# Convolution block, image loop: the output stores moved from SyncE's queue to ScalarE's

## Chip, cores, metric

One Trainium2 chip, one of its cores. The metric is the device time of one execution in microseconds (us); the median of three runs is quoted. All other times are from one profiled execution, counted from the start of its span.

## What is computed

The input `x` has 8 images of 64 channels of 224 x 224 float32. Cut to what matters:

```python
x = x + conv_block(group_norm(x, 32 groups))
# inside conv_block:
res = conv3x3(x, W_id, b_id)                      # all 8 images
# image 0 alone: wavelet split, two attentions, conv3x3 over 256 channels
out = leaky_relu(conv3x3(dmt, W_enc, b_enc), 0.01)   # one map, shape (1, 64, 224, 224)
return out + res                                  # the map is added to every image
```

## The kernel before, in words

The program has three stages, one after another on every engine: `before_maps` (statistics of image 0, weights, row filter), `encoder` (the one map of image 0, kept in SBUF as `e_map`, and the statistics of the other images) and `main` (the image loop, lines 1425 to 1694). The change touches `main` alone. It runs from about 795 us to the end.

**Tiling of `main`.** An image is cut into `NB` = 14 bands. A band has 8 rows of the upper and 8 rows of the lower half of the image: channels of the upper half lie on partitions 0 to 63, those of the lower half on 64 to 127. With the halo a band is 10 rows of 224 elements per partition. The 8 images make 112 bands, numbered n = 14 i + b. Band n goes through these steps:

- `load` (L1488, DMAs at L1499): two DMAs of 64 x 2240 float32 (560 KB) bring the band to `xs[slot]`. There are six slots: bands 1 to 12 share four of them in turn, band 0 has one and band 13 has one of its own.
- `high` and `full` on ScalarE (L1511, L1518): the float16 high part of the normalized band, and the whole of it in float32. `high` of band n waits until the convolution of band n - 2 is through (`tiles`). `split` on VectorE (L1522) makes the float16 low part.
- `conv` on TensorE (L1587): 216 matmuls of 64 x 64 by 448 columns. TensorE's program is written out for all 112 bands; those of SyncE, ScalarE, VectorE and GpSimd are a hardware loop over the images.
- `read_out` on VectorE (L1654): eight instructions scale the PSUM tiles and add `x` from `xs`; each counts `evac` up by one. They write `stage[b % 2]`, and wait first until the store of band n - 2 has landed (`stored`).
- GpSimd (L1681) adds `e_map` in four instructions per band; each counts `added` up by one.
- `store` (L1616): when all four additions are done, four DMAs of 224 KB write the band out.

**SyncE's order.** SyncE issues all transfers of the loop in the written order store(b), load(b + 4). ScalarE issues none. Here `AHEAD` is 4:

```python
for b in range(NB):
    store(i, b)
    load(sp, i, b + AHEAD) if b + AHEAD < NB else load(sp, i + 1, b + AHEAD - NB)
```

**What a load waits for.** Besides its place in the queue, a load waits for the read-out of the band that was last in its slot (`last_band`, L1482):

```python
if b in (TOP, BOTTOM):
    return NB * i + b - NB
return NB * i + b - 4 if b > 4 else NB * i + b - 6
```

So bands 5 to 12 wait for the read-out of bands 1 to 8 of the same image; bands 13 and 0 wait for that of their namesake one image before; bands 1, 2, 3 and 4 wait for that of bands 9, 10, 11 and 12 of the image before. The first loads (bands 0 to 3 of image 0) are issued at the end of the encoder's part of SyncE, and the first two bands are also prepared there.

Of the kernel before, what the change touches and what calls it, by code (L numbers as in the profile page):

```python
# [15 lines left out]
B, C, H, W = 8, 64, 224, 224  # L16
# [10 lines left out]
NB = HALF // R  # L27
# [131 lines left out]
def conv_preact(nc, t, out):  # L159
# [4 lines left out]
    with ExitStack() as top:  # L164
# [29 lines left out]

        with ExitStack() as mid:
            images, ahead = main(nc, x, out, psum, sb, sem, top, pool_of, early, e_map, partner, mv_all, norm_all, w_hi, w_lo, w_max)
            shared = [sb(mid, f"shared{k}", [P, NI * 3 * C]) for k in range(2)]
            weff = [m[:, :].bitcast(F16).rearrange("p (s i y e) -> p s i y e", s=2, i=NI, y=3) for m in shared]
# [1226 lines left out]
def main(nc, x, out, psum, sb, sem, top, pool_of, early, e_map, partner, mv_all, norm_all, w_hi, w_lo, w_max):  # L1425

    with ExitStack() as s5:
# [17 lines left out]
        stage = [sb(s5, f"stage{i}", [P, 2, 2, NT]) for i in range(2)]  # L1445
# [19 lines left out]
        added = sem(top, "added")  # L1465
        stored = [sem(top, f"stored{i}") for i in range(2)]
# [8 lines left out]
        def slot_of(b):  # L1475
            return {TOP: 4, BOTTOM: 5}.get(b, (b - 1) % 4)
# [5 lines left out]
        def last_band(i, b):  # L1482
# [5 lines that stand above are left out]
        def load(sp, i, b):  # L1488
            slot = slot_of(b)
            sp.wait_ge(evac, 8 * (NB + last_band(i, b) + 1))  # L1490
            for s in (1, 0):
                lo_row, hi_row = 0, RH
                if b == TOP and s == 0:
                    lo_row = 1
                if b == BOTTOM and s == 1:
                    hi_row = RH - 1
                row0 = HALF * s + R * b - 1
                src = x[bass.ds(i, 1), :, row0 + lo_row:row0 + hi_row, :]
                sp.dma_start(xs[slot][C * s:C * s + C, lo_row * W:hi_row * W],  # L1499
                             src.rearrange("a c h w -> (a c) (h w)")).then_inc(x_in[slot], 16)  # L1500

        def take_norm(act, i):
            act.wait_ge(xn_ready, NB * i + 1)
            act.copy(norm_now, norm_all[:, bass.ds(i, 1), :].rearrange("p a b -> p (a b)")).then_inc(norm_taken, 1)
            act.wait_ge(norm_taken, i + 1)
# [5 lines left out]
        def high(act, i, b):  # L1511
            n, p, slot = NB * i + b, b % 2, slot_of(b)
            act.wait_ge(x_in[slot], 32 * uses(i, b) + 32)
            act.wait_ge(tiles, 2 * n + 2)
            act.activation(x_hi[p][:, :, 1:1 + W], xs[slot].rearrange("p (r w) -> p r w", w=W), ACT.Identity,  # L1515
                           scale=norm_now[:, 0:1], bias=norm_now[:, 1:2]).then_inc(hi_ready, 1)

        def full(act, i, b):  # L1518
            act.wait_ge(lo_ready, NB * i + b + 1)
            act.activation(xn, xs[slot_of(b)], ACT.Identity, scale=norm_now[:, 0:1], bias=norm_now[:, 1:2]).then_inc(xn_ready, 1)  # L1520
# [92 lines left out]
            pool.tensor_tensor(root, gvar, half7, ALU.pow).then_inc(root_ready, 1)  # L1613

        def sync(sp):
            def store(i, b):  # L1616
                p = b % 2
                sp.wait_ge(added, 4 * (NB * i + b) + 4)
                for s in range(2):
                    for k in range(2):  # L1620
                        row0 = HALF * s + R * b + 4 * k
                        dst = out[bass.ds(i, 1), :, row0:row0 + 4, :]
                        sp.dma_start(dst.rearrange("a c h w -> (a c) (h w)"), stage[p][C * k:C * k + C, s, :, :].rearrange("c g n -> c (g n)"))\
                          .then_inc(stored[p], 16)

            AHEAD = 4
            with sp.Fori(0, B - 1) as i:
                for b in range(NB):
                    store(i, b)
                    load(sp, i, b + AHEAD) if b + AHEAD < NB else load(sp, i + 1, b + AHEAD - NB)  # L1630
            for b in range(NB):
                store(B - 1, b)
                if b + AHEAD < NB:
                    load(sp, B - 1, b + AHEAD)
            for p in range(2):
                sp.wait_ge(stored[p], 64 * (B * NB // 2 + 1))

        def scalar(act):
            def prep(i, b):
                high(act, i, b)  # L1640
                full(act, i, b)

            act.wait_ge(normed, 1)
            with act.Fori(0, B - 1) as i:
                for b in range(2, NB):
                    prep(i, b)
                take_norm(act, i + 1)
                for b in range(2):
                    prep(i + 1, b)
            for b in range(2, NB):  # L1650
                prep(B - 1, b)

        def vector(dve):
            def read_out(i, b):  # L1654
                n, p, slot = NB * i + b, b % 2, slot_of(b)

                dve.wait_ge(stored[p], 64 * (n // 2 if isinstance(n, int) else 7 * i + b // 2) + 64)
                for g in range(2):
                    dve.wait_ge(tiles, 2 * n + g + 5)
                    for r in range(2):  # L1660
                        for k in range(2):
                            o, lanes = slice(C * k, C * k + C), slice(C * r, C * r + C)
                            c = (1 + 4 * k + 2 * g) * W
                            dve.scalar_tensor_tensor(stage[p][o, r, g, :], psum[4 * p + 2 * g + r][o, 0:NT], w_max[lanes, 0:1],  # L1664
                                                     xs[slot][lanes, c:c + NT], ALU.mult, ALU.add).then_inc(evac, 1)

            with dve.Fori(0, B - 1) as i:
                for b in range(NB):
                    read_out(i, b)
                    split(dve, i, b + 2) if b + 2 < NB else split(dve, i + 1, b + 2 - NB)  # L1670
            for b in range(NB):
                read_out(B - 1, b)
                if b + 2 < NB:
                    split(dve, B - 1, b + 2)
# [6 lines left out]
        def gpsimd(pool):  # L1681
            with pool.Fori(0, B) as i:
                for b in range(NB):
                    n, p = NB * i + b, b % 2
                    for g in range(2):
# [6 lines left out]
        ahead = Ahead(load=lambda sp, b: load(sp, 0, b), dummies=dummies, pads=pads, norms=norms, norm_first=first_norm,  # L1692
                      high=high, full=full, split=split, edges=edges, root=root_of, partners=partners, conv=conv)
        return Programs(sync, tensor, scalar, vector, gpsimd), ahead


# [40 lines left out]
```

## Time and profile before

| what | value |
|---|---|
| median of three runs | 1970.77 us (1967.54 to 1971.35) |
| the profiled execution: its time | 1965.66 us |
| its span | 1963.7 us |
| busy TensorE (PE) | 1934.4 us, 99% |
| busy VectorE (DVE) | 1464.4 us, 75% |
| busy ScalarE (ACT) | 1008.3 us, 51% |
| busy GpSimd (POOL) | 1032.8 us, 53% |
| data DMA queue (q1) | 387.10 MB, 77.2% of 16 engines |
| instruction DMAs (q8) | 278 packets, 4.55 MB |

How to read it: PE is TensorE's matmuls and PEld its weight loads, which overlap them; SPq is SyncE's queue of DMA issues. An idle time is put down to what ended it; "issue" means that nothing the profile knows of did. PEclk is the share of full clock that TensorE was granted. q1 holds the data that SyncE's DMAs move, q8 the packets that bring instructions to the engines.

### The profile page before, as it was taken

Reading aid. Unit: us, or ns where it says so; the run is one execution under the profiler, and the core shown is the slowest. Engines: PE = TensorE matmul, PEld = TensorE weight load, DVE = VectorE, ACT = ScalarE, POOL = GpSimd, SP = SyncE. Lnnn points to the kernel's source line nnn. Section 1 sums busy time; section 2 is a strip of 40 time slices with the busy share of each in tenths; the row PEclk is TensorE's granted clock in tenths of the full one; section 3 lists DMA queues with packets and bytes.
Section 4 is the critical chain, followed back from the end, with each engine's and each line's share of the span. In section 5 each row is a group of like instructions: output and inputs, shape, how many; then the busy total and the mean of one; then the engine's idle time right before and its main releaser. Section 6 shows DMA issues by size and latency. Waiting matters only on the chain.

```text
span 1963.7 us, 79515 instructions
## 1 busy us (share of the span) xinstructions
PE 1934.4 (99%) x35530; PEld 1609.5 (82%) x35530; DVE 1464.4 (75%) x2253; ACT 1008.3 (51%) x1067; POOL 1032.8 (53%) x775
## 2 busy tenths in 40 slices
PE   8999999999999999999999999999999999999998
PEld 7987999999999999668897888767877778766664
DVE  5665578778878876577777777777777777777776
ACT  4555666666666676634444344434444444444432
POOL 0005878887888885444444444444444444444444
PEclk9999999999999999999999999999999999999999
DMA  8883598888888884588888877887887878877774
GB/s 172 238 289 98 166 276 214 218 214 216 209 219 215 209 215 104 134 202 205 198 205 208 199 204 197 207 200 194 201 210 198 200 202 206 204 201 199 206 207 124
DMA packets 132647, 391.92 MB, mean 200 GB/s; under 512 B 49676, under 2 KB 50448, under 8 KB 118128
## 3 DMA queue, kind: packets, MB, share of 16 engines
q1 hardware_dynamic: 132336, 387.10, 77.2%
q8 instruction: 278, 4.55, 1.0%
q14 instruction: 33, 0.27, 0.1%
HBM read 258.56 MB, written 128.45 MB: 197 GB/s over the span
## 4 chain that ended last, share of the span: by engine, by line
PE 36%; issue 33%; POOL 26%; ACT 1%; DVE 1%; DMA 1%; POOLq 1%; SPq 0%; DVEq 0%; ACTq 0%
POOL stage L1689 26%; PE ps L1097 13%; PE ps L1063 7%; PE ps L621 5%; PE ps L1067 5%; PE ps L1066 3%; PE ps L623 3%; POOLq L1687 1%; DMA big<-in_x 1%; DVE pool_of L1284 0%; DVE pool_of L1272 0%; DMA pool_of<-in_x 0%; POOL pool_of L1358 0%; POOL pool_of L315 0%; POOL pool_of L306 0%
## 5 line engine op out<-in xcount | busy, mean ns | idle before, releaser
L1689 POOL TENSOR_TENSOR stage<-stage,big 128x448 f32<-128x448 f32 x448 | 511.5, 1142 | 642.7 <-DVE stage L1664 639.9
L1601 PE MATMUL ps<-pool_of,w_hi 64*64 64x448 f16 x12096 | 645.9, 350 | 3.7 <-issue 3.3
L1601 PEld LDWEIGHTS ps<-pool_of,w_hi 64*64 64x64 f16 x12096 | 450.4, 107 | 147.3 <-issue 8.7
L1601 PE MATMUL ps<-pool_of,w_lo 64*64 64x448 f16 x8064 | 452.4, 350 | 2.2 <-issue 2.2
L1601 PEld LDWEIGHTS ps<-pool_of,w_lo 64*64 64x64 f16 x8064 | 304.5, 107 | 98.3 <-issue 4.8
L1664 DVE SCALAR_TENSOR_TENSOR stage<-ps,w_max,pool_of 64x448 f32<-64x448 f32 x448 | 305.9, 683 | 45.7 <-PE ps L1601 33.0
L1284 DVE BATCH_NORM_STATS2 pool_of<-big 128x6 f32<-128x448 f32 x392 | 232.5, 617 | 76.8 <-DMA big<-in_x 76.6
L1515 ACT ACTIVATE pool_of<-pool_of 128x2240 f16<-128x2240 f32 x56 | 126.4, 2258 | 313.9 <-PE ps L1601 313.9
L1664 DVE SCALAR_TENSOR_TENSOR stage<-ps,w_max,xs 64x448 f32<-64x448 f32 x384 | 262.1, 683 | 33.5 <-PE ps L1601 22.1
L1515 ACT ACTIVATE pool_of<-xs,pool_of 128x2240 f16<-128x2240 f32 x48 | 108.4, 2258 | 284.4 <-PE ps L1601 284.4
L1601 PE MATMUL ps<-big,w_hi 64*64 64x448 f16 x4032 | 225.4, 350 | 0.0
L1063 PE MATMUL ps<-pool_of 112*128 112x246 f16 x1344 | 218.8, 271 | 1.0 <-DVE d_odd L1272 0.5
L1067 PE MATMUL ps<-pool_of 112*128 112x168 f16 x1344 | 217.8, 243 | 0.0
L1526 DVE TENSOR_TENSOR big<-pool_of 128x2240 f16<-128x2240 f32 x56 | 139.8, 2496 | 93.4 <-ACT pool_of L1520 93.4
L1526 DVE TENSOR_TENSOR pool_of<-pool_of 128x2240 f16<-128x2240 f32 x56 | 139.7, 2495 | 90.7 <-ACT pool_of L1520 90.7
L1066 PE MATMUL ps<-pool_of 112*128 112x90 f16 x1344 | 201.3, 206 | 0.0
L1601 PEld LDWEIGHTS ps<-big,w_hi 64*64 64x64 f16 x4032 | 153.4, 107 | 46.2
L621 PE MATMUL ps<-fh,pool_of 112*112 112x238 f32 (+1 forms) x512 | 145.6, 366 | 10.8 <-DMA pool_of<-in_x 8.3
L1097 PE MATMUL ps<-pool_of,shared 128*64 128x224 f16 x3024 | 148.4, 259 | 1.2 <-issue 1.2
L1097 PE MATMUL ps<-d_odd,shared 128*64 128x224 f16 x3024 | 148.3, 259 | 0.9 <-issue 0.6
L1097 PEld LDWEIGHTS ps<-pool_of,shared 128*64 128x64 f16 x3024 | 143.7, 110 | 3.0 <-issue 1.4
L1097 PEld LDWEIGHTS ps<-d_odd,shared 128*64 128x64 f16 x3024 | 143.8, 110 | 2.6 <-issue 0.8
(197 smaller groups left out, 2487.4 us busy)
## 6 DMA issues: line engine op xcount, KB each, us to landing
out<-stage SPq DMA_DIRECT2D x448, 224.0 KB, 3.2
big<-in_x SPq DMA_DIRECT2D x392, 224.0 KB, 5.2
pool_of<-in_x SPq DMA_DIRECT2D x104, 560.0 KB, 7.0
xs<-in_x SPq DMA_DIRECT2D x96, 560.0 KB, 7.1
pool_of<-row_filtered SPq DMA_DIRECT2D x110, 224.0 KB, 3.8
pool_of<-in_x SPq DMA_DIRECT2D x32, 392.0 KB, 7.4
row_filtered<-big SPq DMA_DIRECT2D x2, 6272.0 KB, 22.7
row_filtered<-big SPq DMA_DIRECT2D x4, 1568.0 KB, 8.9
```

The source lines that it names most:

```text
L621: pe.matmul(o[:, 0:width], xg[g][:, near, c % CG, :], fh[:, near, first:first + width], start=True, stop=False)
L623: pe.matmul(far_out, xg[g][:, far, c % CG, :], last_rows(fh[:, far, :], first, reach), start=False, stop=True).then_inc(product, 1)
L1063: pe.matmul(tiles(o)[:, :, 15:NTILE], lhs[:, 1, a, :], tiles(v)[:, :, 15:NTILE], start=(k == 0), stop=False)
L1066: pe.matmul(tiles(o)[:, :, 0:15], lhs[:, 0, a, :], tiles(v)[:, :, 0:15], start=False, stop=False)
L1067: mm = pe.matmul(both(o), lhs[:, 0, a, :], both(v), start=False, stop=(k == 2))
L1097: mm = pe.matmul(o[s], weff[a][:, sw, i, ky, :], d[n][:, b, r:r + 4, sw, NTILE * i:NTILE * i + NTILE], start=(k == 0), stop=(k == len(piec ...
L1284: ins = dve.bn_stats(records[:, 2 * (k % CHN) + i, :], sx[k % 4][:, i * NT:i * NT + NT])
L1515: act.activation(x_hi[p][:, :, 1:1 + W], xs[slot].rearrange("p (r w) -> p r w", w=W), ACT.Identity, scale=norm_now[:, 0:1], bias=norm_now[ ...
L1526: ins = dve.tensor_tensor(x_lo[p][:, :, 1:1 + W], xn.rearrange("p (r w) -> p r w", w=W), x_hi[p][:, :, 1:1 + W], ALU.subtract)
L1601: mm = pe.matmul(psum[4 * p + 2 * g + r][C * k:C * k + C, 0:NT], w[lanes, t, :], v[lanes, y:y + 2, kx:kx + W], start=(j == 0), stop=(j == ...
L1664: dve.scalar_tensor_tensor(stage[p][o, r, g, :], psum[4 * p + 2 * g + r][o, 0:NT], w_max[lanes, 0:1], xs[slot][lanes, c:c + NT], ALU.mult, ...
L1689: pool.tensor_tensor(stage[p][:, r, g, :], stage[p][:, r, g, :], e_map[:, e:e + NT], ALU.add)\
```

## The change

ScalarE issues the stores, from its own DMA queue. Those of band b - 2 stand behind `high` and `full` of band b; the last two bands of an image stand behind the preparation of the next image's bands 0 and 1, and those of the last image stand at the end. SyncE's loop holds the loads alone, in the same order as before, and its last waits for `stored`. Buffers, semaphores, DMA shapes and every wait of a load and of a store are unchanged.

```diff
         def sync(sp):
+            AHEAD = 4
+            with sp.Fori(0, B - 1) as i:
+                for b in range(NB):
+                    load(sp, i, b + AHEAD) if b + AHEAD < NB else load(sp, i + 1, b + AHEAD - NB)
+            for b in range(AHEAD, NB):
+                load(sp, B - 1, b)
+            for p in range(2):
+                sp.wait_ge(stored[p], 64 * (B * NB // 2 + 1))
+
+        def scalar(act):
             def store(i, b):
                 p = b % 2
-                sp.wait_ge(added, 4 * (NB * i + b) + 4)
+                act.wait_ge(added, 4 * (NB * i + b) + 4)
...
-                        sp.dma_start(...)
+                        act.dma_start(...)
                           .then_inc(stored[p], 16)
-            AHEAD = 4
-            with sp.Fori(0, B - 1) as i:
-                for b in range(NB):
-                    store(i, b)
-                    load(sp, i, b + AHEAD) if b + AHEAD < NB else load(sp, i + 1, b + AHEAD - NB)
...
             with act.Fori(0, B - 1) as i:
                 for b in range(2, NB):
                     prep(i, b)
+                    store(i, b - 2)
                 take_norm(act, i + 1)
                 for b in range(2):
                     prep(i + 1, b)
+                    store(i, NB - 2 + b)
             for b in range(2, NB):
                 prep(B - 1, b)
+                store(B - 1, b - 2)
+            for b in range(NB - 2, NB):
+                store(B - 1, b)
```

## Rows read from the trace of the kernel before

**Rows 1.** The page's head, and its PE and PEld rows: busy us, instructions

```profile
span 1963.7 us, 79515 instructions
...
PE 1934.4 (99%) x35530; PEld 1609.5 (82%) x35530; DVE 1464.4 (75%) x2253; ACT 1008.3 (51%) x1067; POOL 1032.8 (53%) x775
...
q8 instruction: 278, 4.55, 1.0%
```

**Rows 2.** Waits between 830 and 1964 us: total us, times, longest us

```profile
ACT pool_of L1515 <- PE ps L1601: 636.1, 108, 7.3
...
PE ps L1601 <- issue: 3.5, 7, 1.1
```

**Rows 3.** Timeline of one band: start us, us, engine, line, what

```profile
1200.37 2.26 ACT L1515 ACTIVATE pool_of<-xs,pool_of 128x2240 f16<-128x2240 f32 x1 [5.84 <-PE ps L1601]
1200.38 2.83 DVE L1664 SCALAR_TENSOR_TENSOR stage<-ps,w_max,pool_of 64x448 f32<-64x448 f32 x4 [0.45 <-PE ps L1601]
...
1202.54 2.24 ACT L1520 ACTIVATE pool_of<-xs,pool_of 128x2240 f32<-128x2240 f32 x1
...
1203.28 1.14 POOL L1689 TENSOR_TENSOR stage<-stage,big 128x448 f32<-128x448 f32 x1 [0.29 <-DVE stage L1664]
...
1204.58 2.53 SPq L1623 DMA_DIRECT2D out<-stage  x4
1204.81 2.49 DVE L1526 TENSOR_TENSOR pool_of<-pool_of 128x2240 f16<-128x2240 f32 x1 [1.60 <-ACT pool_of L1520]
...
1207.34 2.83 DVE L1664 SCALAR_TENSOR_TENSOR stage<-ps,w_max,xs 64x448 f32<-64x448 f32 x4
1207.42 1.30 SPq L1499 DMA_DIRECT2D pool_of<-in_x  x2
...
1210.62 2.26 ACT L1515 ACTIVATE pool_of<-big,pool_of 128x2240 f16<-128x2240 f32 x1 [5.84 <-PE ps L1601]
```

**Rows 4.** SyncE's store line: count, ns min/median/max of one

```profile
L1623 SPq DMA_DIRECT2D out<-stage x448: 466/518/1814, 812.8 to 1960.1; - x150
L1623 SPq FUSED_REGOPS  x392: 37/37/48, 812.6 to 1815.6; - x196
L1623 SPq MOVE out<-stage x392: 29/29/38, 812.7 to 1815.7; - x196
```

**Rows 5.** DMA view, 830 to 1964 us: packets, MB, share; issues, us to landing

```profile
q1 hardware_dynamic: 52294, 222.58, 77.9%
q8 instruction: 184, 3.01, 1.2%
...
out<-stage SPq DMA_DIRECT2D x440, 224.0 KB, 3.2
...
xs<-in_x SPq DMA_DIRECT2D x92, 560.0 KB, 7.0
```

**Rows 6.** DMA view, 792.9 to 804.2 us, then 804.2 to 806 us

```profile
q1 hardware_dynamic: 234, 1.76, 71.4%
issues: line engine op xcount, KB each, median us to landing
pool_of<-in_x SPq DMA_DIRECT2D x2, 560.0 KB, 6.3
xs<-in_x SPq DMA_DIRECT2D x2, 560.0 KB, 11.4
...
q8 instruction: 1, 0.02, 4.7%
```

**Rows 7.** Windows after 805.2 us: length, busy us (x count), PEclk, DMA share

```profile
805.20:807.20 2.00, 0.01 (x3) 0.00 (x0) 0.00 (x0) 1.41 (x3) 0.31 (x1) 1.00 0.79 161
807.20:810.70 3.50, 3.50 (x40) 1.87 (x44) 2.08 (x4) 2.17 (x2) 2.62 (x3) 0.51 0.03 10
810.70:820.00 9.30, 9.30 (x204) 5.75 (x199) 5.96 (x7) 2.31 (x3) 3.86 (x4) 1.00 0.61 160
```

**Rows 8.** PE at 1321 us; DMA view, 1309.1 to 1318.4, then 1318.4 to 1320

```profile
1321.31 0.76 PE L1601 MATMUL ps<-pool_of,w_hi 64*64 64x448 f16 x11 [1.09 <-issue]
...
q1 hardware_dynamic: 464, 2.03, 90.0%
...
q8 instruction: 1, 0.02, 5.1%
```

**Rows 9.** Encoder, 448 to 466 us: its window, and its DMA view

```profile
448.00:466.00 18.00, 18.00 (x319) 17.45 (x317) 15.14 (x25) 11.92 (x17) 15.18 (x9) 1.00 0.92 220
...
q8 instruction: 2, 0.03, 0.9%
...
big<-in_x SPq DMA_DIRECT2D x16, 224.0 KB, 5.3
```

More of the change, by code:

```diff
@@ L1622, in store @@
                         dst = out[bass.ds(i, 1), :, row0:row0 + 4, :]
-                        sp.dma_start(dst.rearrange("a c h w -> (a c) (h w)"), stage[p][C * k:C * k + C, s, :, :].rearrange("c g n -> c (g n)"))\
+                        act.dma_start(dst.rearrange("a c h w -> (a c) (h w)"), stage[p][C * k:C * k + C, s, :, :].rearrange("c g n -> c (g n)"))\
                           .then_inc(stored[p], 16)
-            AHEAD = 4
-            with sp.Fori(0, B - 1) as i:
-                for b in range(NB):
-                    store(i, b)
-                    load(sp, i, b + AHEAD) if b + AHEAD < NB else load(sp, i + 1, b + AHEAD - NB)
[L1631 to L1638, printed above, removed]
             def prep(i, b):
```

## Prediction

> **What bounds the kernel now.** I read the page's head first: TensorE is busy for 1934.4 of 1963.7 us [rows 1]. In the waits of the image loop ScalarE stands 636.1 us waiting for TensorE's matmuls, and TensorE itself lacks only 3.5 us in seven gaps, all put down to "issue" [rows 2]. The timeline of one band gives the period and everyone's room: ScalarE's `high` starts at 1200.37 and again at 1210.62, so a band takes 10.25 us, all of it matmuls [rows 3]. In phases after the end of a convolution (1200.37 = 0): the read-out ends at 2.8, ScalarE's preparation at 4.4, GpSimd's last addition at 4.05, the stores are issued from 4.2 to 6.7, VectorE's split runs from 4.4 to 6.9, the loads are issued from 7.05 to 8.35, and the next `high` is due at 10.25 [rows 3]. No engine but TensorE sets the pace, and a gain can come only out of TensorE's gaps.
>
> So I looked at what the gaps are. There are 278 instruction packets of 4.55 MB in all, against 2 x 35530 = 71060 matmuls and weight loads [rows 1]: 256 of them per packet, one packet per 6.2 us of the loop (184 in 1134 us, [rows 5]). The packets are TensorE's code. Around the gap at 1320.22 to 1321.31 no code packet starts for 9.3 us while the data queue is 90% busy; one then starts between 1318.4 and 1320, and TensorE goes on [rows 8]. The longest gap, 1.99 us up to 807.2, has the same form: SyncE issues four loads of 560 KB in that stretch, no code packet starts for 11.3 us, one starts behind 804.2 [rows 6]. The loads issued last land after 11.4 us, against 7.0 in the steady loop [rows 5, 6]. **Code waits behind data, and TensorE then waits for code.** 9.3 us without code cost 1.1 us and 11.3 cost 2.0: some 8.2 to 9.3 us between packets are free, that is 2 to 3 us of delay. After the 2-us gap the granted clock was 0.51 (the 1.2 GHz level) for 3.5 us, in which 40 matmuls were done where 204 x 3.5/9.3 = 77 would have been: 37/21.9 = 1.7 us more [rows 7]. One such event costs 2.0 + 1.7 = 3.7 us.
>
> **The change, part by part.**
>
> *Issuing on ScalarE.* Per band four DMA issues with two register instructions each: 4 x (518 + 37 + 29) ns and gaps, 2.53 us in the row [rows 3, 4]. They begin at about 4.4 and end at 6.9; ScalarE has nothing else until 10.25. With SyncE's worst issue, 1814 ns, in all four it would be 7.3 us and end at 11.7, 1.4 us late. I take 2.5 us, hidden under ScalarE's wait of 5.84 us: zero. The copy of the next image's norms moves behind them by as much: zero. The tail has the same four issues behind the same addition: zero. ScalarE's loop body grows by 14 x 12 = 168 issue and register instructions and 14 waits; a pause at its loop's end has 3.3 us of ScalarE's own room. Zero, once per image.
>
> *The new wait on ScalarE.* `added` of band n - 2 now stands ahead of `high` of band n + 1. It is met at 4.4 at the latest and `high` is due at 10.25. VectorE is the one that waits for ScalarE, TensorE behind it (split ends at 6.9, its matmuls start at 10.25). Zero.
>
> *The stores.* Issued 0.2 us later, now beside the loads. They must have landed when VectorE starts to write the same `stage` buffer two bands on, at 6.97 + 10.25 = 17.2; the last goes out at 6.3 and takes 3.2 [rows 3, 5]: 7.7 us of room. Zero, unless a burst (below) holds them.
>
> *The loads, steady part.* What held them was SyncE's store in front. Now only `evac` does: they go out at about 3.0 instead of 7.05. Two loads (1.15 MB) and four stores (0.92 MB) come within 4.1 us. At 252 GB/s of a busy queue (222.58 MB in 77.9% of 1134 us, [rows 5]) 1.0 MB of it is moved by then, so some 1.1 MB or 4.4 us of data stand ahead of a code packet from phase 4.3 to 7.1 and over 3 us until about 8.5, where today this lasts 1.5 to 2 us behind the loads. Today that costs 3.5 us in the loop [rows 2]; two to three times as long a stretch gives 5 more. Bounds: 0 (nothing stalls more) and, with a 0.5-us stall in 4 of 10 bands, 22. I take 8.
>
> *The loads, bursts.* This is the large term. Today the stores pace the loads, one band each. In the new order load 12 waits for the read-out of band 8, and loads 13 and 0 behind it wait for nothing that is still open. Six DMAs, 3.44 MB or 13.7 us of data, are issued within 4 us, once in each of seven images; then nothing for two bands. Four such DMAs cost 3.7 us [rows 6, 7]. The two more are 4.6 us of data. Lower bound 3.7 (what counts is only what the four showed), upper 3.7 + 4.6 = 8.3; a code packet is due every 6.2 us, so one always falls into it. I take the middle, 6: 7 x 6 = 42 us. The last image has only loads 12 and 13 together: 0 to 3.7, I take 2. At the start load 4 follows the four loads of [rows 6] at once, where it stood behind the first store (812.8, [rows 4]): 0 to 4.6, I take 2.
>
> *The sum:* 42 + 2 + 2 + 8 = **+54 us**. The profiled execution took 1965.66 us, 5.1 below the median of 1970.77, so 2019.7 for its like and **2025** for the median. This case's own range: 7 x 3.7 = 26, and less where a burst misses, from 1990; upper 7 x 8.3 + 3.7 + 4.6 + 22 = 88, 2060.
>
> **The rivals.** 0.2% (4 us) is what a measurement can tell from no change.
>
> *A, code gets through: no slowdown, 1971.* In the encoder 18 us at a DMA share of 0.92 pass with two code packets and not one gap of TensorE [rows 9]; so a full queue alone does not starve it. There the DMAs are of 224 KB, and few are outstanding (they land in 5.3 us). If the wait of a code packet is limited by its turn and not by the data queued, bursts cost nothing beyond today's, and two queues may even give it turns sooner. It decides at 2 to 3 us of delay: below that everything is hidden. Then the time is 1971 less 0 to 4. Against it stands the 11.3 us without code behind four loads [rows 6].
> The Trainium skill (DMA: Bandwidth & Descriptors, Queues, rings and completion order) says that each DMA engine goes round-robin between its queue rows, a packet at a time. By that rule a code packet would wait for one packet of each row, and the change would cost nothing; the trace does not agree, with 11.3 us in which none started. I give A 0.24.
>
> *B, faster.* Loads that start 4 us earlier could end the gaps: at most all 3.5 us of [rows 2] and the 3.7 at the start, 1964. It would need the code to wait less with more data queued. 0.04.
> The Trainium skill (Perfetto Trace Analysis, DMA Optimizations) recommends one issuing engine for inputs and another for outputs where there are loops; here no load is waited for, so the rule has nothing to win but these gaps.
>
> *C, ScalarE becomes the bound.* If an issue takes over (10.25 - 4.4)/4 = 1.46 us on it; at 1.81 each 1.4 us x 111 = 155 us, 2126. The median of 518 ns speaks against it. 0.03.
>
> *D, the stores starve.* Behind a burst of 4.4 MB with the stores (17 us) a store could land up to 21 us after the convolution's end, 4 us past VectorE's need; VectorE has 0.45 + 1.60 idle and 3.3 us ahead of TensorE, so it decides at 5. A little beyond it: 2 us x 7, added to the forecast: 2039. 0.04, inside the range.
>
> **How the numbers follow.** The forecast has 0.65, A 0.24, B 0.04, C 0.03, D 0.04. Faster: B, and the edge of A: 0.05. Same: most of A, 0.22. Slower: 0.73. The range goes down to A, 1969, and up to 2062; it leaves out C, B and the ends of the forecast.
>
> **What would show it.** Right: TensorE's "issue" gaps in the loop rise from 3.5 us to 30 or more, the long ones (over 2 us) once per image beside six loads in a row, each followed by a stretch at half clock, with loads landing after 11 us and more; ScalarE's issues at 0.5 to 0.6 us each and its wait for TensorE still about 3 us. Wrong: bursts are there and code packets start among them; or ScalarE's issues are long; or VectorE waits for DMAs to `out`.

## The result, and the profile after

The changed kernel takes 1994.15 us (1990.8 to 1997.0, 4 runs), the kernel before 1969.15 us with its profiled run counted in. The ratio is 1.0125, 95% interval 1.0106 to 1.0145: **25 us slower**, clear of the 0.2% bound. The forecast was 2025 us, +54. The sign and the mechanism came out; the size was twice too large. Of run 8 below one execution in six took 4110 us, which no trace here explains, and its ratio leaves that one out.

The page of the changed kernel, for [rows 1] and the table of before:

```profile
span 1993.8 us, 79515 instructions
...
PE 1943.5 (97%) x35530; PEld 1549.1 (78%) x35530; DVE 1465.9 (74%) x2253; ACT 1008.0 (51%) x1067; POOL 1039.5 (52%) x775
...
q1 hardware_dynamic: 96496, 284.31, 56.5%
q10 hardware_dynamic: 35840, 102.79, 15.5%
q8 instruction: 278, 4.55, 1.0%
```

The stores are now q10, ScalarE's queue. The bytes and the 278 code packets are the same. The profiled execution took 1995.58 us, 29.9 more than that of before. TensorE's busy time is 9.1 us longer for the same 35530 matmuls, and its idle time is 21 us longer.

The waits of the changed kernel in the image loop, 830 to 1994 us (as in [rows 2]: total us, times, longest us):

```profile
POOL stage L1691 <- DVE stage L1666: 652.1, 440, 8.8
ACT pool_of L1515 <- PE ps L1601: 629.1, 106, 10.5
...
PEld ps L1601 <- issue: 37.5, 36, 3.2
PE ps L1601 <- issue: 22.7, 23, 2.8
ACT pool_of L1504 <- issue: 20.9, 7, 3.5
DVE stage L1666 <- DMA out<-stage: 20.7, 7, 4.5
ACT pool_of L1515 <- POOL stage L1691: 13.9, 2, 7.1
```

TensorE's gaps have gone from 3.5 to 22.7 us, all "issue" as before. Its weight loads tell more, since a recorded matmul is 350 ns long and covers part of a gap: theirs went from 9.4 to 37.5, by 28.1, which is nearly all of the 29.9 us between the two profiled executions. (The PEld row of before, over the image loop:)

```profile
PEld ps L1601 <- issue: 9.4, 16, 1.5
```

Two waits are new: VectorE for stores, once per image, and ScalarE's `high` for the additions, twice. The row of L1504 is no wait: the profile doesn't count DMA issues as busy, and ScalarE issues the four stores right in front of the copy of the norms. It is so in all seven images; in image 0:

```profile
935.76 3.18 ACTq L1633 DMA_DIRECT2D out<-stage  x4
...
939.16 0.19 ACT L1504 COPY pool_of<-norm_all 128x2 f32 x1 [3.20 <-issue]
```

The timeline of the changed kernel in the burst of image 0 (columns as in [rows 3]):

```profile
898.54 1.74 SPq L1499 DMA_DIRECT2D xs<-in_x  x2
899.75 2.77 ACTq L1633 DMA_DIRECT2D out<-stage  x4
...
900.54 1.47 SPq L1499 DMA_DIRECT2D big<-in_x  x2
902.32 19.04 SPq L1499 DMA_DIRECT2D pool_of<-in_x  x6
...
910.70 2.85 PE L1601 MATMUL ps<-pool_of,w_hi 64*64 64x448 f16 x55 [0.66 <-issue]
...
914.39 5.68 DVE L1666 SCALAR_TENSOR_TENSOR stage<-ps,w_max,pool_of 64x448 f32<-64x448 f32 x8 [1.67 <-DMA out<-stage]
...
917.01 2.26 ACT L1515 ACTIVATE pool_of<-xs,pool_of 128x2240 f16<-128x2240 f32 x1 [6.82 <-POOL stage L1691]
...
919.76 3.21 PE L1601 MATMUL ps<-pool_of,w_hi 64*64 64x448 f16 x36 [2.79 <-issue]
```

Loads of three bands go out one after another from 898.5 us. TensorE stops twice within 12 us, for 0.66 and 2.79 us. The DMA view of the changed kernel, 898.8 to 907.9 us, and 908 to 916.9 us below it, has no q8 row in either stretch:

```profile
q1 hardware_dynamic: 235, 1.69, 64.2%
q10 hardware_dynamic: 213, 0.65, 25.5%
...
q1 hardware_dynamic: 277, 1.94, 84.4%
q10 hardware_dynamic: 123, 0.34, 16.5%
```

So code packets start at about 907.9 and 917.0, and TensorE goes on 2.8 us behind each. The bursts do in kind what was forecast. Within 28 us of the first load of a burst lie 16.9 of the 22.7 us of the matmuls' gaps and 24.2 of the 37.5 us of the weight loads'. What the bursts did to the landing times shows in the same kernel over the loop:

```profile
out<-stage ACTq DMA_DIRECT2D x441, 224.0 KB, 6.6
...
xs<-in_x SPq DMA_DIRECT2D x92, 560.0 KB, 6.5
...
big<-in_x SPq DMA_DIRECT2D x8, 504.0 KB, 9.6
pool_of<-in_x SPq DMA_DIRECT2D x7, 504.0 KB, 15.2
```

The last row is band 0 of the next image, the third of a burst. Stores land after 6.6 us in place of 3.2 [rows 5]. It is the loads beside them and not the other queue: in run 1, where the loads wait for the stores' issue, they land after 3.1 us from ScalarE's queue too.

### The profile page after: what moved, and what is told of

Same layout as the page of the kernel before. It is cut to its first block, busy times and chain, and to the rows that moved or that the text cites. A ratio compares the mean times of both kernels' runs of the same rounds, so it can differ in the third digit from the quotient of the medians.

```text
span 1993.8 us, 79515 instructions
## 1 busy us (share of the span) xinstructions
PE 1943.5 (97%) x35530; PEld 1549.1 (78%) x35530; DVE 1465.9 (74%) x2253; ACT 1008.0 (51%) x1067; POOL 1039.5 (52%) x775
## 4 chain that ended last, share of the span: by engine, by line
PE 37%; issue 33%; POOL 26%; ACT 1%; POOLq 1%; DVE 0%; DMA 0%; SPq 0%; DVEq 0%; ACTq 0%
POOL stage L1691 26%; PE ps L1097 14%; PE ps L1063 7%; PE ps L621 5%; PE ps L1067 5%; PE ps L1066 3%; PE ps L623 3%; POOLq L1689 1%; DMA pool_of<-in_x 0%; POOL pool_of L315 0%; POOL pool_of L306 0%; PE ps L587 0%; POOL pool_of L1358 0%; ACT pool_of L1151 0%; PE ps L513 0%
## 5 line engine op out<-in xcount | busy, mean ns | idle before, releaser
L1691 POOL TENSOR_TENSOR stage<-stage,big 128x448 f32<-128x448 f32 x448 | 518.2, 1157 | 662.3 <-DVE stage L1666 659.6
L1601 PE MATMUL ps<-pool_of,w_hi 64*64 64x448 f16 x12096 | 647.0, 351 | 15.2 <-issue 15.1
L1601 PEld LDWEIGHTS ps<-pool_of,w_hi 64*64 64x64 f16 x12096 | 416.2, 107 | 194.3 <-issue 22.2
L1601 PEld LDWEIGHTS ps<-pool_of,w_lo 64*64 64x64 f16 x8064 | 282.9, 107 | 128.4 <-issue 15.3
L1601 PEld LDWEIGHTS ps<-big,w_hi 64*64 64x64 f16 x4032 | 145.1, 108 | 58.6 <-issue 3.9
```

The lines of the kernel that those rows point to most:

```text
L1601: mm = pe.matmul(psum[4 * p + 2 * g + r][C * k:C * k + C, 0:NT], w[lanes, t, :], v[lanes, y:y + 2, kx:kx + W], start=(j == 0), stop=(j == ...
L1691: pool.tensor_tensor(stage[p][:, r, g, :], stage[p][:, r, g, :], e_map[:, e:e + NT], ALU.add)\
```

## The experiments

The three theories: **T1**, bursts of loads hold TensorE's code; **T2**, it is the loads beside the stores in every band; **T3**, it is the second queue, ScalarE's issues or its new wait. Eleven kernels ran. Each ratio is to the kernel before on the same chip, whose median was 1972.3 us for the first four runs, 1970.0 for the next four and 1968.9 for the last three. The diffs are cut to the image loop: the same edits for the last image, and in runs 3 and 7 a load of band 4 ahead of the loop, are left out.

**1. The second queue alone.** The loads wait until ScalarE has issued the stores of the band.

```diff
                 for b in range(NB):
+                    sp.wait_ge(issued, NB * i + b + 1)
                     load(sp, i, b + AHEAD) ...
 # ScalarE, behind the four act.dma_start of store(i, b):
+                act.sem_inc(issued, 1)
```

> Changed kernel, but SyncE issues the load of band b + 4 only when ScalarE has issued the stores of band b: loads and stores are in the order and at the times of the kernel before, only the stores' queue and engine differ. Theory T1 (the time went to bursts: six loads in a row once per image keep TensorE's code waiting) and theory T2 (it went to the loads standing earlier, among the stores, in every band) both say: back to the kernel before, 0 to +3 us, no TensorE gap over 1.5 us in the loop. Theory T3 (it is the second queue, ScalarE's issues or the wait for the additions ahead of its preparation) says +15 us or more stays.

Measured: 1970.1 us, ratio 0.9987 (0.9972 to 1.0001). The waits in the loop, 830 to 1950 us:

```profile
ACT pool_of L1505 <- issue: 19.7, 7, 3.6
PEld ps L1602 <- issue: 17.8, 26, 1.5
PE ps L1602 <- issue: 7.4, 11, 1.1
```

T3 falls as a cause by itself. Issuing 448 stores on ScalarE and its wait for the additions are covered, as priced: no gap between TensorE's matmuls is over 1.1 us. (The row of L1505 is again its own store issues, seven times.) None of the 25 us comes without the loads' earlier places. The weight loads' 17.8 us are more than the 9.4 of the kernel before presumably because that one's profile caught one of its shorter executions, 1965.66 us; this one took 1973.38.

**2. Loads early, but one band at a time, two queues.** The load of band b + 4 also waits for the read-out of band b:

```diff
                 for b in range(NB):
+                    sp.wait_ge(evac, 8 * (NB + NB * i + b + 1))
                     load(sp, i, b + AHEAD) ...
```

> Changed kernel, but the load of band b + 4 also waits for the read-out of band b: one band's loads per band, no bursts, still 4 us earlier than before and beside the stores of ScalarE's queue. T1: at most +5 us against the kernel before, where the changed kernel has +25. T2: +15 us or more stays, in many gaps under 1.5 us, evenly over the bands. T3: like T2.

Measured: 1981.1 us, ratio 1.0045 (1.0026 to 1.0063), +9 us: between T1's 5 and T2's 15. The gaps are many, as T2 had it, though some are over its 1.5 us, and they are worth a third of the loss.

```profile
PEld ps L1601 <- issue: 30.4, 39, 2.4
...
PE ps L1601 <- issue: 14.8, 18, 2.0
```

**3. Bursts on one queue.** The kernel before, with the load order that the changed kernel falls into:

```diff
                     store(i, b)
-                    load(sp, i, b + AHEAD) if b + AHEAD < NB else load(sp, i + 1, b + AHEAD - NB)
+                    if 1 <= b <= 8:
+                        load(sp, i, b + AHEAD)
+                    if b == 8:
+                        load(sp, i, BOTTOM)
+                        load(sp, i + 1, TOP)
+                    if 9 <= b <= 12:
+                        load(sp, i + 1, b - 8)
```

> Kernel before, all DMAs on SyncE, but its loads stand in the order that the changed kernel gives them: behind the store of band 8 the loads of bands 12, 13 and 0, none behind the stores of bands 13 and 0. The start is as before. T1: +15 to +25 us, a gap of 2 to 3 us in TensorE once per image; the next store waits behind six loads, so gaps may be longer than in the changed kernel. T2 and T3: within 4 us of the kernel before.

Measured: 1995.0 us, ratio 1.0111 (1.0089 to 1.0134), +22 us. This is T1's own test: ScalarE issues nothing here, stores stand first, and the loss of the changed kernel is there nearly whole. Timeline around the burst of image 1:

```profile
1045.58 1.36 SPq L1499 DMA_DIRECT2D xs<-in_x  x2
...
1047.20 1.53 SPq L1499 DMA_DIRECT2D big<-in_x  x2
...
1049.03 1.66 SPq L1499 DMA_DIRECT2D pool_of<-in_x  x2
...
1056.43 0.95 PE L1601 MATMUL ps<-pool_of,w_hi 64*64 64x448 f16 x14 [1.55 <-issue]
...
1065.25 1.71 PE L1601 MATMUL ps<-pool_of,w_lo 64*64 64x448 f16 x31 [2.56 <-issue]
...
1072.56 0.76 PE L1601 MATMUL ps<-pool_of,w_lo 64*64 64x448 f16 x11 [1.04 <-issue]
...
1079.44 3.23 PE L1601 MATMUL ps<-pool_of,w_hi 64*64 64x448 f16 x63 [0.61 <-issue]
```

Four code packets in a row come late, at 0.6 to 2.6 us each.

**4. Loads early on one queue, no bursts.** The kernel before, the load ahead of the band's store and behind its read-out (band 0 keeps its order):

```diff
+                    if b == 0:
+                        store(i, b)
+                    if b >= 9:
+                        sp.wait_ge(evac, 8 * (NB + NB * i + b + 1))
                     load(sp, i, b + AHEAD) if ... else load(...)
-                    store(i, b)   # stood ahead of the load
+                    if b > 0:
+                        store(i, b)
```

> Kernel before, all DMAs on SyncE, but the load of band b + 4 stands ahead of the store of band b and waits for the read-out of band b (band 0 excepted): no bursts, loads at 3 us instead of 7 us after a convolution's end, the stores behind them in one queue. T1: within 4 us of the kernel before. T2: +10 us or more. T3: within 4 us.

Measured: 1975.0 us, ratio 1.0005 (0.9989 to 1.0021), no difference. Loads 4 us earlier cost nothing on one queue, or at most 4 us by the interval. Experiment 2 has nearly the same load times, so the 0.4% between them goes with the second queue: where the loads are early it has a price, which it has not in run 1. That it is because the stores are not kept behind the loads there is a guess; it wasn't taken further.

**5 and 6. TensorE without code to fetch.** TensorE's program for bands 2 to 111 becomes a loop over pairs, on the changed kernel (5) and on the kernel before (6). The increment only gives the waits an instruction of their own:

```diff
-            for n in range(1, B * NB):
-                conv(pe, n, n % 2)
+            conv(pe, 1, 1)
+            with pe.Fori(1, B * NB // 2) as m:
+                for p in range(2):
+                    conv(pe, 2 * m + p, p)
 # in conv, behind its three waits, inside the loop:
+                pe.sem_inc(nopped, 1)
```

> Changed kernel, but TensorE's program for bands 2 to 111 is a hardware loop over pairs of bands, 864 matmuls and weight loads long, instead of being written out. If TensorE can run the loop from instructions it already holds, the image loop needs almost no code packets (some 90 to 100 in all instead of 278). Theory T1 (code packets held behind bursts of loads) then says: the 25 us of the change are gone although loads, stores and queues are as in the changed kernel, within 5 us of the same loop on the kernel before, plus whatever the loop's own branch costs (55 times). Rival T3 (second queue, late stores, waits on ScalarE) says the distance of 20 us or more to that kernel stays. If the packets are fetched all the same at each turn, the packet count stays near 278 and the run tells nothing but that.

> Kernel before with the same loop over pairs of bands on TensorE. It gives the loop's own price: if code is kept, the gaps of 3.5 us in the loop go and each of 55 turns may cost 0 to 2 us, 1965 to 2080 us. The number wanted is its distance to the changed kernel with the same loop.

Measured: 1963.2 us (ratio 0.9960, 0.9948 to 0.9973) with the changed kernel's DMAs and 1958.7 us (0.9940, 0.9926 to 0.9954) with those of before. The distance between the two is 4.5 us in place of 25. Run 6 came out below the 1965 us that was expected at least, since the waits for code were worth more than 3.5 us. The page of run 5, its DMA view from 830 to 1950 us, then its waits there:

```profile
q8 instruction: 96, 1.57, 0.4%
```

```profile
pool_of<-in_x SPq DMA_DIRECT2D x7, 504.0 KB, 14.6
```

```profile
ACT pool_of L1516 <- POOL stage L1696: 92.3, 11, 9.1
...
ACT pool_of L1516 <- issue: 25.3, 3, 8.7
DVE stage L1669 <- DMA out<-stage: 22.8, 7, 3.6
...
PEld ps L1604 <- issue: 3.0, 4, 1.0
PE ps L1604 <- DVE big L1535: 1.2, 3, 0.6
```

This settles the cause. Bursts (the third load lands after 14.6 us, 15.2 in the changed kernel), second queue and late stores (22.8 us of VectorE's time) are all still there; only the code packets are gone, 96 in place of 278, and with them 20 of the 25 us. TensorE runs a loop of two bands from what it holds, and the loop's 55 turns cost less than the waits they save. The remaining 4.5 us weren't taken apart by a run, but the list shows where they may lie: 3.0 us of gaps in the weight loads, and 1.2 us of TensorE waiting for VectorE, neither of which run 6 has in the loop. The second comes from the stores: VectorE waits for them, the additions are late, and ScalarE, which now waits for these (92.3 us in eleven waits, and three more where `high` starts right behind its late issues), prepares the next band late.

**7. A smaller burst.** One queue; the loads of bands 12 and 13 stand together, and every later load one band earlier than before. The diff is against run 3:

```diff
                     if b == 8:
                         load(sp, i, BOTTOM)
-                        load(sp, i + 1, TOP)
-                    if 9 <= b <= 12:
-                        load(sp, i + 1, b - 8)
+                    if b == 9:
+                        load(sp, i + 1, TOP)
+                    if 10 <= b <= 13:
+                        load(sp, i + 1, b - 9)
```

> Kernel before, all on SyncE, with a smaller burst once per image: the loads of bands 12 and 13 together behind the store of band 8, every later load one band earlier than in the kernel before. Bursts of three bands cost 22 us. T1: the price follows the length of the burst: a burst of 9 us of data instead of 13.7 holds one or two code packets less, +5 to +13 us. If instead the price hung on anything that such an order brings at all (loads further ahead of their use), it would be 20 us or more, or nothing.

Measured: 1979.3 us, ratio 1.0044 (1.0029 to 1.0059), +9 us. A burst of two bands costs 9 us, one of three 22 (per image 1.2 and 3.1 us): the price follows the length, and grows faster than the length. That this is because the first packet's wait is mostly free is plausible, but wasn't shown.

**8. The loads drawn apart.** The kernel before; of a band's two load DMAs one stands ahead of the stores and one behind:

```diff
-                    store(i, b)
-                    load(...)
+                    if b == 0:
+                        store(i, b)
+                    if b >= 9:
+                        sp.wait_ge(evac, 8 * (NB + NB * i + b + 1))
+                    half(i, b, 1)          # load DMA of s = 1
+                    if b > 0:
+                        store(i, b)
+                    half(i, b, 0)          # load DMA of s = 0
```

> Kernel before, all on SyncE, with the two load DMAs of a band drawn apart: one ahead of the band's four stores, as soon as the band is read out, one behind them. T1: never more than about 0.6 MB of loads stand in a row, so code packets are held less: the gaps in the loop fall below 3.5 us, and the time by 0 to 4 us. If data anywhere in the queue counts alike, it is like the run with both loads ahead of the stores: 0 to +3 us.

Measured: 1958.1 us, ratio 0.9934 (0.9920 to 0.9949), **12 us faster than the kernel before**, where 0 to 4 were expected. The code is still fetched, the bytes are the same, and the wait is gone. The page and the waits in the loop, 830 to 1950 us:

```profile
q8 instruction: 278, 4.55, 1.0%
```

```profile
PEld ps L1602 <- issue: 0.4, 1, 0.4
```

**9. The same on the changed kernel.** Stores from ScalarE; first load DMA behind the read-out, the second behind ScalarE's issues, in 12 of 14 bands. The diff is against run 1:

```diff
-                    sp.wait_ge(issued, NB * i + b + 1)
-                    load(...)
+                    if b in (0, 10):
+                        sp.wait_ge(issued, NB * i + b + 1)
+                    elif b >= 9:
+                        sp.wait_ge(evac, 8 * (NB + NB * i + b + 1))
+                    half(i, b, 1)
+                    if b not in (0, 10):
+                        sp.wait_ge(issued, NB * i + b + 1)
+                    half(i, b, 0)
```

> Changed kernel (stores from ScalarE's queue), its loads paced one band per band, and the two load DMAs of a band drawn apart in 12 of 14 bands: the first when the band is read out, the second when ScalarE has issued the stores. On one queue this split gave 1958 us, ratio 0.993. T1 (only what stands in a row ahead of the code counts): 0.993 to 0.997 here too, with two bands of 14 left unsplit. T3 (the second queue costs by itself): 1.000 or more.

Measured: 1960.4 us, ratio 0.9947 (0.9929 to 0.9965). The change's idea, stores on ScalarE, gains nothing, and costs nothing where the loads are paced (run 1) or drawn apart (this run); with early loads that go out together it does cost (run 2 beside run 4). With it in place, the order of the loads is worth 0.5% one way and 1.25% the other.

**10 and 11. Both cures, and the start.** Run 10 puts runs 6 and 8 together; run 11 also holds one load at the start:

```diff
 # encoder, SyncE:
-            for b in range(2, 4):
-                ahead.load(sp, b)
+            ahead.load(sp, 2)
 # main, ahead of the loop:
+            sp.wait_ge(tiles, 5)
+            load(sp, 0, 3)
```

> Kernel before with the split loads and the loop over pairs of bands on TensorE together. Both remove the same waits for code, so T1 says they don't add: within 2 us of either alone, 1956 to 1960. If they acted on different things the time would be near 1947.

> As the run with the split and the loop, and the load of band 3 of image 0 is held until half of the first convolution is through, so that only two of the loads at the start stand in a row. T1: the gap of 2 us of TensorE near 807 us shrinks, 1 to 4 us less than without this, 1953 to 1958.

Measured: 1958.1 us (0.9941, 0.9925 to 0.9956) and 1956.9 us (0.9933, 0.9918 to 0.9948). The cures don't add up, so they remove the same waits. The start's 1.2 us lie inside the intervals: inconclusive by the time. In the traces the weight loads' gap between 795 and 830 us is 1.1 us in run 10 and gone in run 11, where the kernel before has 4.0.

## Why the prediction was right in kind and wrong in size

- **What bounds the kernel, and what the gaps are.** Right: TensorE, stopped only by its code, behind data. Runs 5 and 6 show it. But the gaps were read too small. They were taken from the PE row, 3.5 us [rows 2], where the PEld row had 9.4, and taking them away (run 8) gave 12 us for the whole kernel. Rival B's bound of 1964 us was therefore too high, though B itself did not come.
- **Issues on ScalarE, the new wait, the moved copy, the tail: zero.** Right (run 1). An issue took 496 ns in the changed kernel against 518 on SyncE [rows 4], and the four in front of the copy 2.4 to 3.5 us. Only the new wait was not always met at 4.4: behind a burst `high` waited for the additions, twice in the changed kernel, without TensorE waiting for it.
- **ScalarE's loop end: zero.** Right. No pause shows there: in the first image `high` behind the loop's end starts at 962.86 us, after the usual 5.84 us of idle time.
- **The bursts, 42 us.** This is the step that failed. Their price was put at 3.7 to 8.3 us each and 6 was taken, as if a code packet waited for all data ahead of it and each stop brought a slow stretch. Run 3 gives 22 us for seven, 3.1 each (2.5 to 3.8 by its interval), and in the changed kernel's own trace the weight loads lack 24.2 us beside the seven bursts, 3.5 each. Two terms of it were mis-sized. *The wait:* the burst's last load was issued at 903.0 and landed 16.0 us later, and before that two code packets had started, at 907.9 and 917.0: one of the prediction's own signs of being wrong. The stretches without a code packet were 9.1 us, shorter than the 11.3 behind four loads [rows 6], although about 13 us of data were queued (3.33 MB and not 3.44, as two of the six loads are of 504 KB; they were issued within 5 us, not 4). A longer burst makes more packets late, not one packet later: in run 3 two to four per image, 2.3 to 5.8 us together by the matmul rows. What lets a code packet through after some 9 us stays open. *The clock:* 1.7 us were added to every stop. Stops over 2 us came in three of seven images, of 2.79, 2.82 and 2.02 us. The windows behind them show half clock twice, and run 3 has none beside its bursts, not even behind a stop of 2.56 us (the last row, of run 3; columns as in [rows 7]):

```profile
919.10:922.50 3.40, 2.74 (x32) 1.73 (x35) 2.00 (x3) 2.31 (x2) 1.89 (x2) 0.50 1.05 339
1072.70:1076.10 3.40, 3.40 (x43) 2.18 (x36) 1.37 (x1) 0.00 (x0) 2.36 (x1) 0.50 1.01 249
1513.70:1517.10 3.40, 3.40 (x73) 2.58 (x76) 3.33 (x3) 0.69 (x1) 3.06 (x2) 1.00 0.74 219
...
1046.00:1071.00 25.00, 20.90 (x438) 14.36 (x434) 17.64 (x22) 8.81 (x4) 9.93 (x9) 1.00 1.00 255
```

- **The steady part, 8 us.** Run 2, without bursts, measured 9, but the changed kernel doesn't show as much: away from its bursts the weight loads lack 13.3 us, 3.9 more than in the whole loop of before. The reason given was only half of it: the same load times on one queue cost nothing (run 4). The sum of runs 2 and 3 is 31 us against 25 measured. That they don't add is plausible, since the changed kernel issues no loads beside two bands of each image, but wasn't shown.
- **The start and the last image, 2 + 2.** No run separates them, and the traces show no such loss: between 795 and 830 us the weight loads lack 3.9 us in place of 4.0, the half clock of [rows 7] doesn't come, and the last image has one stop of 0.4 us.
- **Rival A** (code gets through a full queue) is refuted as stated, but its argument, that a code packet's wait is limited by something else than the data queued, was the right correction to the forecast. Its evidence stood in [rows 9]. **The round-robin rule of the Trainium skill** (DMA: Bandwidth & Descriptors, Queues, rings and completion order) would have given no change; the 9.1 us without a code packet up to 917.0, followed by a stop of TensorE of 2.79 us, don't agree, though the profile doesn't show when the packet was asked for. **Rival D** began to show: VectorE waited for stores once per image, up to 4.5 us, short of the 5 at which TensorE would feel it. In run 5, with waits up to 3.6 us, TensorE did feel it, by 1.2 us in three images: the limit was set too high. The way goes over the additions and ScalarE's new wait for them: near 1357 us of run 5 `high` starts after 8.98 us of idle time in place of 5.84, and VectorE's split waits 3.73 us for ScalarE, where it waited 1.6. **Rival C** did not come.

## What to carry to other kernels

When an engine runs straight-line code, its instruction packets are traffic, and gaps put down to "issue" may be waits for them: look in the DMA view for a missing instruction row in the stretch before each gap. A queue that holds unrelated stores may be what spaces the loads; before moving them away, ask which loads then have nothing left to wait for, and give each a wait of its own. Issuing a band's two loads apart, with its stores between them, or a loop short enough to be kept, was worth 0.6% here; either was enough.

## What was not expected of the hardware

- TensorE's loop over two bands, 864 matmuls and weight loads, brought no code packets: between 830 and 1950 us run 6 has 2, the kernel before 184.
- With the DMA engines busy all the time, two queues moved somewhat more than one: 279 GB/s in the changed kernel's first burst (900 to 925 us), 255 in a burst of run 3 on one queue (1046 to 1071 us). These are single bursts.
- A stop of 1.99 us was followed by half clock in the kernel before [rows 7], one of 2.02 us in the changed kernel and one of 2.56 us in run 3 were not.
